# Experts on the chosen pairs alone: 31 sorted tiles of plain fp32 products in place of 44 tiles of split products over all 512 tokens

## What is computed

```python
xn = _layernorm(x)
x = x + _L0_attn_ref(xn, ...) + _L0_ffn_ref(xn, topk_idx, ...)   # ffn: E, H, I, TOPK = 16, 512, 352, 4

flat_expert = topk_idx.reshape(-1)                 # 512 tokens x 4 choices = 2048 pairs
perm = jnp.argsort(flat_expert)
xs = x[tok]                                        # the token of each pair, sorted by expert
gate = ragged_dot(xs, gate_weight); up = ragged_dot(xs, up_weight)
down = ragged_dot(silu(gate) * up, down_weight)
out = zeros.at[tok].add(down * w_sorted[:, None])
```

## Time and profile before

| | |
|---|---|
| median of 3 runs | 3481.83 us (3479.11 to 3482.67) |
| the profiled execution | 3482.47 us, span 3480.9 us, granted clock 0.995 |
| PE / DVE / ACT / POOL busy | 98% / 68% / 67% / 55% of the span |
| first matmul of the experts | 15.35 us |
| first matmul of `heads` | 417.25 us |
| memory read and written | 292.62 MB, 76.58 MB |

### The profile page before, as it was taken

One profiled execution on the slowest core, in us unless ns is written; L12 is line 12 of the kernel. 1 busy time (PEld: TensorE's weight loads), 2 busy tenths in 40 slices (PEclk: granted clock), 3 DMA queues, 4 the chain that ended last, 5 costly groups with the idle time before them and its releaser, 6 DMA issues. The chain is left out here.

```text
span 3480.9 us, 105791 instructions
## 1 busy us (share of the span) xinstructions
PE 3426.1 (98%) x32308; PEld 2900.5 (83%) x32308; DVE 2353.1 (68%) x5785; ACT 2348.0 (67%) x6448; POOL 1921.0 (55%) x4905
## 2 busy tenths in 40 slices
PE   8999989999999999999999999999999999999999
PEld 6788768888888888888888888888888888877887
DVE  6656557777777777777777777777777777742222
ACT  4443367777777777777777777777777777752111
POOL 3333256666666666666666666666666666653000
PEclk9999999999999999999999999999999999999999
DMA  8654433333333333333543333333333333444443
GB/s 306 232 179 165 168 93 78 81 79 85 83 90 78 81 79 86 82 78 80 152 108 85 78 78 81 80 86 81 78 81 78 84 88 88 124 140 132 144 145 105
DMA packets 427674, 375.83 MB, mean 108 GB/s; under 512 B 191984, under 2 KB 323056, under 8 KB 421248
## 3 DMA queue, kind: packets, MB, share of 16 engines
q1 hardware_dynamic: 424000, 362.46, 39.0%
q0 software_dynamic: 2080, 6.82, 0.5%
q10 hardware_dynamic: 1056, 0.02, 0.0%
HBM read 292.62 MB, written 76.58 MB: 106 GB/s over the span
## 5 line engine op out<-in xcount | busy, mean ns | idle before, releaser
L1332 DVE SCALAR_TENSOR_TENSOR conv<-bank,tap,conv 128x512 f32<-128x512 f32 x1152 | 854.6, 742 | 57.0 <-ACT conv L1468 47.0
L1158 POOL TENSOR_TENSOR prods<-Lb,Tc 128x60 f32<-128x60 f32 (+14 forms) x1920 | 482.3, 251 | 622.0 <-DMA Lb<-base_d 486.7
L1540 PE MATMUL bank<-hx_hi,w_lo 128*128 128x512 f32 x1536 | 652.1, 425 | 11.1 <-DVE Tnb L1294 11.1
L1540 PE MATMUL bank<-hx_hi,w_hi 128*128 128x512 f32 x1536 | 655.7, 427 | 0.8 <-DVE conv L1332 0.8
L1540 PE MATMUL bank<-hx_lo,w_hi 128*128 128x512 f32 x1536 | 637.1, 415 | 0.0
L1165 POOL TENSOR_TENSOR Tc<-Tc,prods 128x56 f32<-128x56 f32 (+13 forms) x1792 | 462.3, 258 | 140.3
L1540 PEld LDWEIGHTS bank<-hx_hi,w_lo 128*128 128x128 f32 x1536 | 292.3, 190 | 43.2 <-DVE Tnb L1294 12.4
L1540 PEld LDWEIGHTS bank<-hx_hi,w_hi 128*128 128x128 f32 x1536 | 293.1, 191 | 29.3 <-DVE conv L1332 0.9
L1540 PEld LDWEIGHTS bank<-hx_lo,w_hi 128*128 128x128 f32 x1536 | 292.4, 190 | 29.9
L1286 DVE SCALAR_TENSOR_TENSOR S<-S,gamma,bank 128x128 f32<-128x128 f32 x480 | 166.0, 346 | 191.8 <-PE bank L1653 186.1
L1273 DVE SCALAR_TENSOR_TENSOR R<-bank,scale_c,v_rows 128x128 f32<-128x128 f32 x480 | 164.1, 342 | 189.0 <-PE bank L1629 188.9
(11 more groups left out here) (211 smaller groups left out, 8833.9 us busy)
## 6 DMA issues: line engine op xcount, KB each, us to landing
Lb<-base_d SPq DMA_DIRECT2D x128, 512.0 KB, 4.8
gamma<-gamma_d SPq DMA_DIRECT2D x128, 258.0 KB, 4.3
alpha<-alpha_d SPq DMA_DIRECT2D x128, 256.0 KB, 3.2
oT_d<-oG SPq DMA_DIRECT2D x128, 256.0 KB
gu_raw<-in_gate_up SPq DMA_DIRECT2D x16, 1408.0 KB, 6.4
o_raw<-oT_d SPq DMA_DIRECT2D x13, 1024.0 KB, 6.9
w_raw<-oT_d SPq DMA_DIRECT2D x12, 1024.0 KB, 6.8
dn_raw<-in_down SPq DMA_DIRECT2D x44, 256.0 KB, 6.7
```

Source lines behind the costliest of these rows:

```text
L1158: pool.tensor_tensor(prods[:, :, i + 1:], Lb[:, i, :, i + 1:], Tc[:, :, i:i + 1].to_broadcast([P, G, SB - 1 - i]), ALU.mult)\
L1332: dve.scalar_tensor_tensor(out=conv[i][:, to], in0=PJ[PJ_OF[g][i]][:], scalar=tap[:, i, j + 1:j + 2], in1=conv[i][:, to], op0=ALU.mult, op ...
L1540: last = pe.matmul(dst, a[:, i, k], b[:, k], start=(j == 0), stop=(j == 3 * KC - 1))
```

## The change

It replaces the experts' part of `prepare`:

- **Routing on the chip.** From the 2048 choices VectorE and two matmuls count the pairs of each expert and give each expert as many tiles of 128 pairs as it needs. `TILES_E` = 2048/128 + 15 = 31 tiles are run, whatever the counts. `expert` holds each tile's expert (SP reads it into a register), `taken` each tile's tokens, `share` their weights, `place` where each pair's result lies.
- **A tile.** GpSimd gathers 128 rows of normalised x from memory (`xn_d`, 256 KB), TensorE transposes them (`turn_x`), ScalarE copies them. Gate and up are 24 plain fp32 products with 128 pairs moving, down is 3 with 512 columns moving. Nothing is split. The result, times its share, is stored to `y_d` (256 KB).
- **Weights.** Every tile loads its expert's gate and up (`gu`) and down (`dn`) whole, also when the tile before had the same expert. There are 4 buffers of each, and loads are issued three tiles ahead.
- **x** of the groups has two buffers, and a group takes four tiles (`group(t)`); Wo's four parts stand at tiles 4, 9, 14 and 19.
- **`project`** gathers the four results of each of the 512 tokens (16 gathers of 256 KB) and adds them to x, in place of adding `moe` from SBUF.

The core of the diff (declarations, the removed splits and the unchanged arithmetic of the groups left out):

```diff
+TILES_E = GT * TOPK // P + E - 1
+RAW = 4
+            def load_gate_up(t, e):
+                wait(sp, up_done, t - RAW + 1)
+                sp.dma_start(gu[:, t % RAW], gate_up[bass.ds(e, 1)].rearrange("o (p k) n -> p (o k) n", k=KC)).then_inc(gu_loaded[t % RAW], 16)
+            def load_down(t, e):
+                wait(sp, down_done, t - RAW + 1)
+                wait(sp, const_built, CONSTANTS)
...
+            def expert_of(t):
+                wait(sp, routed, done("expert"))
+                return sp.value_load(expert[0:1, t:t + 1], min_val=0, max_val=E - 1)
...
+            for t in range(TILES_E + 2):
+                if t + RAW - 1 < TILES_E:
+                    e = expert_of(t + RAW - 1)
+                    load_gate_up(t + RAW - 1, e)
+                g, phase = group(t)
+                if phase == 0:
+                    if g + 1 < NG:
+                        load_x(g + 1)
+                    store(g - 1)
...
+                if t >= 2:
+                    wait(sp, y_done, t - 1)
+                    sp.dma_start(y_d[(t - 2) * P:(t - 1) * P, :], y[:, t % 2]).then_inc(y_stored[t % 2], 16)
...
+                if t + RAW - 1 < TILES_E:
+                    load_down(t + RAW - 1, e)
...
+            def gather(t):
+                wait(pool, xg_turned, t - 1)
+                pool.indirect_dma_start(out=xg[:, t % 2], out_offset=None, in_=xn_d,
+                                        in_offset=bass.IndirectOffsetOnAxis(ap=taken[:, t:t + 1], axis=0),
...
+            for t in range(TILES_E + 2):                       # ScalarE
+                if t >= 2:
+                    wait(act, down_done, t - 1)
+                    wait(act, y_stored[t % 2], 16 * (t // 2 - 1))
+                    act.activation(y[:, t % 2], Y[t % 2][:], ACT.Copy, scale=share[:, t - 2:t - 1]).then_inc(y_done, 1)
...
+            def gate_or_up(t, part, dst):
+                for c, n in enumerate(INNER):
+                    inner = slice(part * I + c * P, part * I + c * P + n)
+                    for k in range(KC):
+                        last = pe.matmul(dst[0:n, c * P:(c + 1) * P], gu[:, t % RAW, k, inner], xgT[:, t % 2, k],
...
+            def add_down(t):
+                wait(pe, dn_loaded[t % RAW], 2 * nth(t))
+                wait(pe, h_done, t + 1)
+                wait(pe, y_done, t - 1)
+                for c in range(3):
+                    last = pe.matmul(Y[t % 2][:], h[:, t % 2, c * P:(c + 1) * P], dn[:, t % RAW, c], start=(c == 0), stop=(c == 2))
...
+            for i in range(GT // P):                           # project, GpSimd
+                for k in range(TOPK):
+                    c = i * TOPK + k
+                    pool.indirect_dma_start(out=picked[:, i, k], out_offset=None, in_=y_d,
...
```

More of the change, by code:

```diff
@@ L259, in back @@
[L259 to L293, removed]
@@ L301, in prepare, with done @@
+        STEPS_OF = ("index", "match", "upto", "more", "ahead", "tiles", "end", "past", "begin", "number", "expert", "rank", "offset",
+                    "own", "slot", "reached", "in_tile", "whole", "inside", "weight", "row", "place", "taken", "share")
+        def done(step):
+            return STEPS_OF.index(step) + 1
         block = ctx.enter_context(nc.Block())
@@ L305, in load_x @@
             def load_x(g):
[L306 to L334, removed]
+                wait(sp, turned, (g - 1) * TT)
@@ L675, in gates, with turn_x @@
                 last.then_inc(z_done, 1)
-            def gate_or_up(r, u, part, dst):
-                s = slot(u)
+            def turn_x(t):
+                wait(pe, gathered[t % 2], 16 * (t // 2 + 1))
+                wait(pe, xg_copied, t)
+                columns = xg[:, t % 2].rearrange("p (n k) -> p k n", k=KC)
                 for k in range(KC):
-                    pe.matmul(dst[:], gu_hi[:, s, k, part], x_hi[:, k], start=(k == 0), stop=False)
-                    pe.matmul(dst[:], gu_hi[:, s, k, part], x_lo[:, k], start=False, stop=False)
-                    last = pe.matmul(dst[:], gu_lo[:, s, k, part], x_hi[:, k], start=False, stop=(k == KC - 1))
-                return last
@@ new lines, in _ @@
+            wait(pe, const_built, 7)
+            wait(pe, routed, done("match"))
+            pe.matmul(BEFORE, tri[:, 0], match[:].rearrange("p e c -> p (e c)"), start=True, stop=True)
+            pe.matmul(TOTAL, tri[:, 1], match[:].rearrange("p e c -> p (e c)"), start=True, stop=True).then_inc(counted, 1)
+            turn_tiles(0, range(TT))
+            wait(pe, fill_done, 1)
+            wait(pe, routed, done("row"))
+            for c in range(PICKS):
+                last = pe.matmul(TABLE, at_row[:, c], fill[:, c].rearrange("p v t -> p (v t)"), start=(c == 0), stop=(c == PICKS - 1))
@@ L715, in turn @@
+            last.then_inc(table_done, 1)
+            gates(0)
+            wait(pe, routed, done("rank"))
+            turn_x(0)
+            wait(pe, routed, done("share"))
+            for t in range(TILES_E + 1):
+                if t < TILES_E:
+                    wait(pe, gu_loaded[t % RAW], nth(t))
+                    wait(pe, xg_copied, t + 1)
                     wait(pe, gated_done, t)
-                    gate_or_up(r, u, 0, GATE).then_inc(gate_done, 1)
+                    gate_or_up(t, 0, GATE).then_inc(gate_done, 1)
+                if t + 1 < TILES_E:
+                    turn_x(t + 1)
+                if t < TILES_E:
@@ L717, in turn @@
                     wait(pe, h_done, t)
-                    gate_or_up(r, u, 1, UP).then_inc(up_done, 1)
-                    for g, first in groups(r):
-                        if begun(g) and u in (first + 2, first + 3):
-                            turn_tiles(g, (0, 1) if u == first + 2 else (2, 3))
-                        if u == first + 4:
-                            if isinstance(g, int) and g == 0:
-                                wait(pe, routeT_done, 1)
-                            gates(g)
```

574 lines of the change are left out of this document (290 added, 284 removed).

## The result

The changed kernel took 3454.3 us (median of 4 runs, 3450.66 to 3455.08), the kernel before 3481.93 us beside it. The ratio is 0.9921, with a 95% interval of 0.991 to 0.9933: 28 us faster, where the forecast was 64 us. The profiled execution took 3455.08 us, with a span of 3453.5 us.

What follows compares the result with a forecast made beforehand. TensorE, busy 98%, bound the kernel; after the change the DMA engines would bind the first stage. `heads` would start at 353 instead of 417.25 us, a gain of 64: 3482.5 - 64 = 3418 us, range 3396 to 3464.

Steps and rivals of the forecast that it cites:

- TensorE's 8.4 us a tile: First stage: gate and up, transposes and down together take TensorE 8.4 us a tile, 260 us for 31.
- 297 and a tail of 5: First stage: TensorE needs 297 us where it needed 400, with 5 us of tail before `heads` if TensorE decides.
- The first weights at 16 us, 370 GB/s and the last `gu` at 337 us: First stage: transfers bind; 118.8 MB at 370 GB/s take 321 us from 16 us, so the last gate and up land at 337.
- First expert product at 34 us: First stage: after routing, normalisation, table, gates and gather, the first expert product comes at 34 us, against 15.35.
- Most of the stop lies in TensorE's slack: First stage: TensorE stops some 10 us in each group, mostly hidden (DMA engines 45 us a group, TensorE 38); cost nothing.
- runs dry at both ends: Rival, first stage, 13%: stops and waits add, 2 to 5 us in each of 8 groups; gain 20 to 45 us.
- The tail of 16 us behind the last `gu`: End of first stage: last gate and up, down, y copy and store follow the last load; `heads` starts at 353 us.
- `heads` carried over unchanged: `heads`: own work and same inputs after the change, so its 2770 us were kept.
- `project` and its gathers at nothing: `project`: four gathers are there after 8 us, within TensorE's 10.9 us a tile; cost 0.
- The clock: Rival, first stage, chance within other cases: clock falls with the waits, 2.5 us of TensorE's slack a group, cannot feed on itself.

Runs made afterwards that it cites:

- no_reload: The changed kernel without the loads of gate_up and down from the fifth tile on, the first four tiles' weights used for all 31: 3423.58 us.
- both: The changed kernel with GpSimd's gather ahead of the group's power, and xT_hi and xT_lo in two buffers: 3447.44 us, ratio 0.9915.
- the pair on slot 0: The changed kernel with ScalarE's `heads` loop on slot 0, without (3432.06 us) and with gather ahead of the power and two xT buffers (3422.3 us).
- the other three profiles of its stage: Profiles of the changed kernel with ScalarE's `heads` loop begun on slots 0, 208 and 64, stage unedited: `heads` began at 370.8, 372.3 and 369.9 us.
- all_y4: The changed kernel with gather ahead of the power, two xT buffers, four y buffers and ScalarE's `heads` loop on slot 0: 3421.88 us, ratio 0.9837.
- down_two: all_y4 with two of the three down products of a tile, all transfers kept: `heads` began at 351.22 us.
- slot 0 or 64: The changed kernel with ScalarE's `heads` loop begun on that slot of a block of 256 instructions: 3432.06 us (0), 3432.18 us (64).
- slot 208: ScalarE's `heads` loop begun on slot 208 of a block of 256 instructions: 3497.53 us in the kernel before, 3456.95 us in the changed kernel.
- 148: The kernel before with ScalarE's `heads` loop begun on slot 148 of a block of 256 instructions: 3481.77 us, ratio 1.0009.

## Why the prediction failed, point by point

- **TensorE's 8.4 us a tile**: right. 24 starts of L681 are 0.111 us apart a pass, six passes of L690 take 2.74 us, and in `no_reload` 299.8 us pass from the first expert product (40.31 us) to `heads`, where the forecast had 297 and a tail of 5.
- **The first weights at 16 us, 370 GB/s and the last `gu` at 337 us**: right to some 2% as a capacity. The first packet of `gu` came at 15.7 us. The changed kernel reached 362 GB/s (last packet at 341.5 us), and 369 GB/s (336.7 us) with the stops' causes removed. The Trainium skill (DMA: Bandwidth & Descriptors, "Where 436 GB/s comes from") puts one core at about 358 GB/s; stretches of 50 us ran at 373 to 376 in the changed kernel and at up to 381 in `both`, so the measurement decides.
- **First expert product at 34 us**: 39.48. The table (L701, 16 products in 32 passes of 62 columns) took 7.06 us and had no number of its own in the forecast. The granted clock was 0.50 meanwhile, so a pass took 0.22 us, twice the 0.111 of full clock; the first six of the 12 `gates` products behind it followed each other at some 0.43 us for the same reason. The first gather was issued at 31.13 us and used at 37.98, where issue and landing had 4 us. The DMA engines are full meanwhile, so this costs nothing where the transfers bind; it does count where TensorE decides, as at the end of the changed kernel.
- **"Most of the stop lies in TensorE's slack"**: the first step that failed. The forecast had seen the stop and its 10 us, and set it against 7 us of slack in each group (45 us of transfers against 38 of TensorE). By its own sizes only the four groups with a part of Wo have that slack. The three without are 14.0 MB each, 37.9 us at 370 GB/s, as long as TensorE's 38. Over the whole stage it had TensorE ready by its own path at 336 us (34 + 297 + 5), 17 us before the transfers' 353. Measured, TensorE began 5.5 us late, waited 30.0 us where 5 were allowed (13.5 on the take, 12.3 on gathers, which the forecast had at nothing: a gather landed after 7.5 us, less than a tile, but was issued late), and was busy some 12 us longer by the clock. Together 42.5 us, less the forecast's 5 us of tail, which the waits contain: 38 us, 21 more than the 17. The other side agrees: removing the two causes of stops gave back 11.5 to 13.7 us of the stage (9.9 us in the pair on slot 0), less than their 25.8 us, since the transfers then bound it. The rival "runs dry at both ends" had this mechanism, stops that add. It gave the stage a gain of 20 to 45 us; the stage gained 43.4, which alone would have made some 3438 us. That the time lies in the middle of its 3437 to 3462 us is luck, since the rest of the way is `heads`, which it did not have.
- **The tail of 16 us behind the last `gu`**: 32 us in the changed kernel (30 to 32 in the other three profiles of its stage), 22 to 24 with the stops removed. The forecast let TensorE catch up with the last load. But the last three tiles carry no group: 2.69 MB of weights, gather and store for a tile are 7.3 us at 370 GB/s (an estimate), less than TensorE's 8.4, so the loads run ahead and TensorE has two or three tiles left. In `all_y4` its last wait for `gu` ends at 291.76 us, inside the first tile of the last group, which has no part of Wo either; `down_two` with shorter tiles has a tail of 15.5 us. Both agree, but no run tested the loads' lead by itself. These 6 to 8 us over the forecast's 16 are the rest of the stage's 21 us.
- **"`heads` carried over unchanged"**: the second step that failed, 15.9 us. Its instructions and data are the same; the place of ScalarE's code is not, and ScalarE stood for some 2 us at every jump back. This was shown in both kernels: the loss goes with slot 0 or 64 in the changed one and comes with slot 208 in the kernel before.
- **`project` and its gathers at nothing**: right, 292.5 against 292.4 us.
- **The clock**: 0.94 from 16 to 335 us. It fell after stops, as forecast, and did not feed on itself: each spell ended after 3.4 to 6.8 us. But its price of some 12 us stood in no sum of the forecast, which had put it into the same slack.

Stage 20.9 us and `heads` 15.9 us make 36.8 us; the median is 36.3 us above the forecast. The parts come from one profile each, so the 0.5 us between them mean nothing. What stays open is how the code lies in the changed kernel as loaded: slots 0 and 64 cost nothing in the changed kernel, 148 nothing in the kernel before, and 208 costs in both; by count the jump back lies on slot 2 of a block with 208. No further slot was tried, so "just behind the start of a block" is the reading that fits four points and no more.

The Trainium skill (Runtime: NRT & Kernel Launch, "Instruction fetch mechanics") says that a taken branch to code outside a two-page window forces a fetch of the target page before execution goes on. The transfers around the waits agree. But this body of 1074 instructions is longer than two blocks of 256 wherever it lies, and with slots 0, 64 and 148 the jump cost nothing that these traces show. The loop is written with `hint_back_edge=True` in all of them, and no run left that out.

## What to carry to other kernels

When a change brings a second engine near the first one's load, a stop no longer hides in the average slack: compare the sum of all late starts, stops and slow clock behind them with the slack of the whole stage, group by group, and price stores and gathers by their landing under full DMA engines (stores took 13.5 to 17.3 us here, against 5.7 us in the earlier trace rows). Work out the tail by which of the two is slower in the last tiles, not on average. A stage that is "unchanged" still moves in memory: look for waits on "issue" once per iteration of a long unrolled loop, and fix the place of its code on every engine, not only on TensorE.

## What the runs showed that was not expected

At a jump back ScalarE stood idle for 1.7 to 2.5 us or not at all, by the place of its code alone. Nine of them cost `heads` 14.6 us in the kernel before (2786.9 against 2772.3) and 22.6 us in the changed one (2787.1 against 2764.5), where TensorE was also busy 10 us longer (2747.1 against 2737.1), in part at the lower clock. Doubling y's buffers removed 17.8 us of TensorE's waits on ScalarE and gave nothing, since 19.8 us of waits for weights came in their place.
